# Other signals ahead of the result row gathers and another order of the last one-hot sum, in an attention + MoE kernel

## The reference

```python
x = x + xattn(layernorm(x), ctx_512, ...)        # 16 heads, 512 rows of x, 512 of context
x = x + ffn(layernorm(x), ...)                   # below
# ffn: 32 experts, each token takes its best 4
scores = sigmoid(h @ gate_weight.T); topk_idx, tw = grouped top-4(scores + bias)
routed = sum over experts e of combine[:, e] * (silu(h @ w1[e].T) * (h @ w3[e].T)) @ w2[e].T
out = x + routed + shared_expert(h)
```

## Time and profile before

| | us |
|---|---|
| median of 3 runs (lowest, highest) | 306.88 (306.75, 307.32) |
| the profiled execution | 307.86 |
| its span, first to last instruction | 305.6 |
| TensorE busy in it | 288.5 (94%) |
| result row gathers (L1325), first and last start | 275.1 and 298.2 |
| combine (L641), first start | 272.2 |
| granted TensorE clock, mean | 0.989 of full speed |

### The profile page before, as it was taken

The page is one execution under the profiler, slowest core; times in us unless marked ns, Lnnn a source line. Parts: engine busy times, 40 slices in busy tenths (PEclk is TensorE's granted clock), DMA queues, the critical chain, the costliest instruction groups (busy, mean ns, idle before and its releaser), DMA issues.

```text
span 305.6 us, 5498 instructions
## 1 busy us (share of the span) xinstructions
PE 288.5 (94%) x1847; PEld 204.9 (67%) x1847; DVE 182.0 (60%) x432; ACT 159.1 (52%) x378; POOL 133.4 (44%) x124
## 2 busy tenths in 40 slices
PE   8988899999999999999999999987989999999981
PEld 6665767765778675787657877754556666667661
DVE  4595766657776787766674366148842333342775
ACT  3535877676667667786684265185213333332420
POOL 0661937795009590059960000000166544546571
PEclk9999999999999999999999999999899999999997
DMA  7950006100700000700029991502033445433233
GB/s 233 398 208 1 0 1 201 76 0 2 237 39 2 2 1 0 259 0 3 0 76 363 403 387 53 200 2 69 0 105 104 153 145 153 139 103 86 66 92 103
DMA packets 15850, 34.14 MB, mean 112 GB/s; under 512 B 2512, under 2 KB 8400, under 8 KB 15824
## 3 DMA queue, kind: packets, MB, share of 16 engines
q1 hardware_dynamic: 13520, 27.51, 25.0%
q0 software_dynamic: 2304, 6.29, 7.3%
HBM read 30.12 MB, written 3.67 MB: 111 GB/s over the span
## 4 chain that ended last, share of the span: by engine, by line
PE 87%; DVE 4%; issue 2%; ACT 2%; POOL 2%; DMA 1%; POOLq 0%; DVEq 0%; ACTq 0%
PE bank L572 10%; PE bank L555 9%; PE bank L664 9%; PE bank L546 6%; PE bank L547 5%; PE bank L685 5%; PE bank L526 5%; PE bank L441 4%; PE bank L443 4%; PE bank L442 3%; PE bank L470 3%; PE bank L501 3%; PE bank L653 3%; PE bank L504 3%; PE bank L448 3%
## 5 line engine op out<-in xcount | busy, mean ns | idle before, releaser
L1320 POOL DMA_INDIRECT rope<-xn_rows,idx x32 | 31.2, 974 | 83.4 <-DVE idx L1223 61.9
L347 POOL TENSOR_TENSOR rtmp<-abuf,rope 128x512 f32<-128x512 f32 x21 | 27.3, 1302 | 60.6 <-PE bank L443 41.1
L829 ACT ACTIVATE prob<-bank,nmax 128x512 f32<-128x512 f32 x48 | 32.7, 685 | 36.7 <-DVE nmax L1013 36.7
L1013 DVE TENSOR_REDUCE nmax<-bank 128x1 f32<-128x512 f32 x64 | 41.1, 684 | 6.6 <-PE bank L547 6.0
L664 PE MATMUL bank<-wall,nmat 128*64 (+1 forms) x256 | 31.2, 385 | 0.8 <-issue 0.8
L572 PE MATMUL bank<-pT,kvr 128*64 128x256 f32 x256 | 31.2, 385 | 0.0
L1031 DVE COPY pT<-bank 128x512 f32<-128x512 f32 x32 | 22.0, 687 | 12.3 <-PE bank L555 12.1
L546 PE MATMUL bank<-kdup,qsp 128*128 128x512 f32 x64 | 28.3, 442 | 0.8 <-ACT prob L829 0.8
L985 DVE COPY abuf<-bank 64x512 f32<-64x512 f32 x24 | 16.4, 684 | 19.5 <-ACT abuf L805 19.2
L350 POOL TENSOR_TENSOR roped<-rtmp 128x512 f32<-128x512 f32 x21 | 27.2, 1295 | 1.6
L348 POOL TENSOR_TENSOR rtmp<-abuf,rope 128x512 f32<-128x512 f32 x21 | 27.4, 1305 | 0.0
(11 more groups left out here) (203 smaller groups left out, 564.5 us busy)
## 6 DMA issues: line engine op xcount, KB each, us to landing
wall<-in_w_exp SPq DMA_DIRECT2D x32, 384.0 KB, 7.3
wring<-in_w_attn SPq DMA_DIRECT2D x16, 224.0 KB, 3.9
wring<-in_w_attn SPq DMA_DIRECT2D x4, 640.0 KB, 8.2
y_rows<-nmat SPq DMA_DIRECT2D x10, 256.0 KB
wring<-in_w_attn SPq DMA_DIRECT2D x4, 512.0 KB, 6.8
rope<-in_rope_q SPq DMA_DIRECT2D x1, 768.0 KB, 6.5
x_sb<-in_x SPq DMA_DIRECT2D x1, 512.0 KB, 3.6
xn_rows<-xn SPq DMA_DIRECT2D x4, 128.0 KB, 1.7
```

What stands on the lines that cost most here:

```text
L347: eng.tensor_tensor(t0.rearrange("p (b s) -> p b s", b=B), own.rearrange("p (b s) -> p b s", b=B), cos, ALU.mult)
L829: act.activation(probs[t % 4], s_ps[t % 3][:, :], ACT.Exp, bias=nmax[:, t:t + 1], accum_out=psum_e[:, t:t + 1]).then_inc(s_exp, 1)
L1013: dve.tensor_reduce(nmax[:, t:t + 1], s_ps[t % 3][:, :], AX.X, ALU.max, negate=True).then_inc(s_max, 1)
L1320: pool.indirect_dma_start(xg[:, u % XG, :], None, xn_dram, bass.IndirectOffsetOnAxis(idx[:, u:u + 1], 0)) \
```

## The change

The result gathers 0 to 11 each get a signal of their own: 0 that of `slot_weights` (`sw_mm`, given once near the start of the loop), 1 to 11 the signals of TensorE in their order. 12 to 15 stay without. The last combine, p = 5, runs over the token tiles in its outer loop, and signals each of the two banks by a new semaphore, `acc_end`. DVE adds the sum's tiles 0 and 1 after gather 13, tile 2 after gather 14, tile 3 ahead of gather 15, whose add becomes the last instruction.

```diff
@@ combine(p)
-                                           start=(p == 0 and i == 0 and hl == 0 and tt % 2 == 0),
-                                           stop=(p == DIR // 2 - 1 and i == 1 and hl == 1 and tt % 2 == 1), skip_group_check=True)
+                                           start=(p == 0 and i == 0 and hl == 0 and tt % 2 == 0), stop=False, skip_group_check=True)
                 mm.then_inc(acc_mm, 1)
+
+            def combine_last(p):
+                pe.wait_ge(yu_ev, NG_U // 2 + p + 1)
+                pe.wait_ge(oh_done, p + 1)
+                for tt in range(TT):
+                    for i in range(2):
+                        for hl in range(2):
+                            mm = pe.matmul(acc_ps[tt // 2][:, (tt % 2) * D:(tt % 2 + 1) * D],
+                                           one_hot[:, p % 2, i, tt * P:(tt + 1) * P], yd[:, p % 2, i, hl, :],
+                                           start=False, stop=(i == 1 and hl == 1 and tt % 2 == 1), skip_group_check=True)
+                    if tt % 2 == 1:
+                        mm.then_inc(acc_end, 1)
@@ TensorE's loop
-                if j - 3 >= NG_U // 2:
+                if j == NU // 2 + 2:
+                    combine_last(DIR // 2 - 1)
+                elif j - 3 >= NG_U // 2:
                     combine(j - 3 - NG_U // 2)
@@ DVE, after its loop
-            add_rows(PACE * (DIR // 2 - 2), NK)
-            dve.wait_ge(acc_mm, DIR // 2)
-            for tt in range(TT):
-                dve.tensor_tensor(x_sb[:, tt, :], acc_ps[tt // 2][:, (tt % 2) * D:(tt % 2 + 1) * D], x_sb[:, tt, :], ALU.add) \
-                   .then_inc(fin, 1)
+            def add_sum(tt):
+                dve.wait_ge(acc_end, tt // 2 + 1)
+                return dve.tensor_tensor(x_sb[:, tt, :], acc_ps[tt // 2][:, (tt % 2) * D:(tt % 2 + 1) * D], x_sb[:, tt, :], ALU.add)
+
+            add_rows(PACE * (DIR // 2 - 2), NK - 2)
+            for tt in range(2):
+                add_sum(tt).then_inc(fin, 1)
+            add_rows(NK - 2, NK - 1)
+            add_sum(2).then_inc(fin, 1)
+            link(add_sum(TT - 1))
+            dve.wait_ge(d_y4[NK - 1], 16)
+            dve.scalar_tensor_tensor(x_sb[:, TT - 1, :], y4[:, TT - 1, TOPK - 1, :], topw[:, 0, TT - 1, TOPK - 1:TOPK], x_sb[:, TT - 1, :],
+                                     ALU.mult, ALU.add).then_inc(fin, 1)
@@ POOL, the result gathers
-            gates = {0: (acc_mm, 1), 1: (yu_mm, G2 + 2), 3: (hu_mm, G2 + 4), 5: (yu_mm, G2 + 3), 6: (hu_mm, G2 + 5), 8: (yu_mm, G2 + 4),
-                     9: (hu_mm, G2 + 6), 11: (yu_mm, G2 + 5)}
+            gates = {1: (acc_mm, 1), 2: (yu_mm, G2 + 2), 3: (hu_mm, G2 + 4), 4: (acc_mm, 2), 5: (yu_mm, G2 + 3), 6: (hu_mm, G2 + 5),
+                     7: (acc_mm, 3), 8: (yu_mm, G2 + 4), 9: (hu_mm, G2 + 6), 10: (acc_mm, 4), 11: (yu_mm, G2 + 5)}
             for i in range(NK):
+                if i == 0:
+                    pool.wait_ge(sw_mm, 1)
                 if i in gates:
                     pool.wait_ge(*gates[i])
                 collect(*divmod(i, TOPK))
```

More of the change, by code:

```diff
@@ L283, in build @@
         d_iota = sem("d_iota"); w_one = sem("w_one"); sw_mm = sem("sw_mm"); sw_done = sem("sw_done")
-        oh_done = sem("oh_done"); yd_hi = sem("yd_hi"); acc_mm = sem("acc_mm")
+        acc_end = sem("acc_end"); oh_done = sem("oh_done"); yd_hi = sem("yd_hi"); acc_mm = sem("acc_mm")
         fin = sem("fin")
```

## The result

The kernel after takes 306.00 us (median of 22 runs, 305.55 to 307.87), the kernel before 307.09 (22 runs, 306.55 to 309.20). The ratio is 0.9962, interval 0.9945 to 0.9979: faster by some 1.1 us. The forecast was 306.0.

The account below looks back on a forecast made before the run. It took gather 15's start, its landing and DVE's and SP's work behind it to bound the end. `acc_end` at 300.1 plus 2.47 puts the fourth output DMA at 302.6, not 303.4: 306.88 - 0.85 = 306.0, range 305.1 to 307.2.

Parts of the forecast that it names:

- Three stretches in series set the end: End of kernel: POOL's start of gather 15, its landing 2.76 us later, then DVE's and SP's work behind it.
- B: Rival: no signal held anywhere; DVE goes on at 299.27, SP starts at 301.75; 1.65 us less, 305.2; chance 0.16.
- the 0.57: TensorE's idling ahead of combine(2), blamed on held signals; to vanish, making all later TensorE steps 0.57 us earlier.
- a fault in the middle: Near 280 to 282 us, TensorE's signals to DVE, ACT and POOL held, one by about 2.2 us.
- upper bound: Arrival of `acc_end` at DVE if held: 1.31 us behind the end of the last back-to-back gather, 300.16.
- lower bound: Arrival of `acc_end` unheld: with TensorE's rows, so at once for DVE at 299.27.
- gather 10's new gate gives back 0.24: On POOL, gather 10 waits for combine(3), so gather 15 starts only 0.33 us earlier, at 297.90.
- The overlap with the hot rows: Gather 10 beside DVE's hot rows takes 1.06 instead of 0.95 us; 0.11 more, left out of the sum.
- A: The forecast itself: the hold at 280 goes, the one at the end stays; 306.0 us; chance 0.42.
- C: Rival: the instruction packet, not the gathers, holds signals at 280; TensorE keeps 0.57 idling; 0.2 less, 306.7; chance 0.20.
- D: Rival: DVE's hot rows lock gathers out for their whole length, up to 0.88 us; no change, 306.9; chance 0.10.
- E: Rival: `acc_end` held past gather 15's transfer, 2.47 us of DVE work queued behind; 0.8 later, 307.7; chance 0.12.

Follow-up runs that it names:

- gates_only: Kernel before with only the new signals ahead of the gathers, old end: 307.85 us against 307.70 on the first chip, 307.88 against 306.95 on the third.
- tail_only: Kernel after with the old gates, so only the last combine by token tile and DVE's new order: 307.10 us on the first chip, before 307.70.
- after_again: Kernel after unchanged, run again on the second chip: 305.89 us against 307.06 for before, ratio 0.9966.
- no_gate10: Kernel after without gather 10's new wait for combine(3), on the second chip: 305.76 us, before 307.06, ratio 0.9970.
- free kernels: Kernel after and kernel before, each with no TensorE signal ahead of gathers 1 to 15: both 324.0 us, ratios 1.0507 and 1.050 to before.
- before_look: Kernel before unchanged, profiled once on the third chip beside three others: 307.66 us in one run.
- more_signals: Kernel after with signals for gathers 12 to 15 too, all nearer together, and DVE's adds moved further forward: 304.73 us, before 307.06, ratio 0.9921.

## Why the prediction was right

The time, 306.0, is right, and so is the piece that carries it: "Three stretches in series set the end", of which DVE's and SP's behind the landing is the removable one. SP's lag of 0.37 us behind DVE went too, as said. Two steps beside it were wrong and cancel, and that the time came out to the tenth is luck. Without holds the forecast's own terms give 1.65 us (B) less the 0.57 that was never there, 1.08; the near groups give 1.05, 1.17 and 1.07 in the three comparisons of after. The forecast had 0.85, because the 0.57 too much nearly made up for the 0.8 that it took off for a held signal at the end. And it counted from 306.88, the median of three runs, 0.21 below that of the 22.

**"I take it that signals are not held there, and the 0.57 us of idling goes."** It goes on a chip that has it (gates_only: no idle before combine(2)). On the second and third chip the kernel before has no such idling, and its times in the first comparison are like those there (306.99 beside 307.06 and 306.95), so there was nothing to gain. My words "a fault in the middle" treated one execution's rows as the kernel's. The same holds for "That execution stood 0.98 above the median of the runs", which I passed over as an offset; the three plain runs were not of its kind.

**"I take a value near the upper bound, 300.1."** The signal of the last combine was there when DVE asked for it, the lower bound: in the profile of after DVE adds the sum at 298.92, right behind its five adds, and the last add ends at 301.37, not 302.57. The idle time of about 0.8 us ahead of the first add of the sum, which was to show the forecast right, is not there. On the chip that holds, the rule of the upper bound was met to 0.01 us (tail_only). So each of the two prices is found on a chip of its kind, and the sum mixed the two.

**"gather 10's new gate gives back 0.24"**: on POOL 0.5 us between after_again and no_gate10, twice the amount, and worth nothing at the end. The overlap with the hot rows that my sum left out cost 0.12 per gather (1.07 against 0.95 us, four times in after); gathers 13 and 14, beside DVE's work as well, took 1.06 and 1.00.

The rivals. A happened in its time and not in its mechanism. B, no signal held, is what the chips of the comparison do; its 305.2 was too low by the 0.57 that was never there. C's mechanism, an instruction packet, is refuted as a sufficient cause, on the chip that holds: in gates_only one ran at 279.2, as before, and the signal of combine(1) came 0.03 us behind its end. (In after one is at 280.9 and one at 295.3, with no hold either.) D: the Trainium skill's rule (SBUF — State Buffer, Who interferes with whom) would let a gather beside hot rows lose up to 0.88 us, if these are two-port instructions. Four gathers that start together with the hot rows took 1.07, never more, so what they lost is a seventh of that. Whether the hot rows ran in such a mode no row says, so this prices the overlap here and does not test the rule. E did not happen; on the holding chip tail_only's signal came 1.3 us behind the last gather, no later, while with sixteen gathers in a row the same mechanism cost 16 us.

What stays open: no profile of the kernel after shows a hold, and no run of it is on record from the first chip, so whether its two parts together bring more than 0.6 us there is not shown. The free kernels were tried on that chip alone; whether they beat after on a chip that holds nothing is untested. What makes a chip hold, no run shows.

## What to carry to other kernels

Look for what stands between the last landing and the last output, and move all that doesn't need the landing ahead of it: that was the whole gain here, 1.1 us where nothing is held. On the chip that holds it was 0.6, in a comparison that does not exclude none (0.9959 to 1.0006). Before a wait in a profile is called the kernel's, look whether the profiled execution lies among the plain runs. That is a hint and no proof: the one of before lay 0.98 us above their median and had a hold, before_look lay 0.55 above (307.66 against 307.11) and had none. A profile of the old kernel beside the new one, on one chip, is the cheapest experiment of all. Signals ahead of gathers are insurance: they bring nothing where nothing is held, and they cost where the last gather is the bound. Set nearer together they let the last gather start sooner, and with the adds moved forward that was the fastest kernel here (more_signals).

## What was not expected

Back-to-back indirect gathers of POOL, 0.95 us each and 0.30 apart, held TensorE's signals to ACT, DVE and POOL on one chip, for 2 us with five gathers (tail_only) and for up to 17.8 with sixteen, while TensorE nearly stopped; the cost was 16 us of 308. DVE's own signals to itself went through: its adds, each of which waits for the one before, kept their pace of 0.525 us while TensorE's signals were held at the end of tail_only (five adds in 2.61 us).

The two groups of executions lie in the granted TensorE clock ahead of the change. Windows of after (near group) and more_signals (its profile is of the far one): us, busy time of the engines, PEclk, DMA share, GB/s.

```profile
217.00:227.00 10.00, 8.63 (x56) 6.56 (x58) 7.49 (x28) 0.59 (x1) 5.58 (x6) 1.00 0.18 53
```

```profile
217.00:227.00 10.00, 9.10 (x45) 7.46 (x44) 8.02 (x29) 0.61 (x3) 4.49 (x4) 0.75 0.14 40
```

PEclk is the mean granted clock. The 0.75 of the second stretch is half at full speed, 2.4 GHz, and half at the lower level, 1.2 GHz; what follows is then as fast as in the first: from the last input gather to the end of the last combine 27.14 us in after (271.47 to 298.61) and 27.15 in more_signals (273.29 to 300.44). In all fourteen profiles the last input gather starts at 271.3 to 271.7 us where PEclk is 0.98 or more in this window, and later where it is less, up to 273.6.
